# Gated expert rows added onto the residual in DRAM by an accumulating scatter, and a last stage that only normalises

## The reference

```
x = layernorm(x + rotor_attention(x))      # values, turned, running sum, turned back, projected
x = layernorm(x + decayed_attention(x, ctx, ctx))
x = layernorm(x + moe(x))

def moe(x):                                # 8 experts, 2 chosen per row
    probs = softmax(x @ router.T); scores, idx = top_k(probs, 2)
    scores = scores / sum(scores)          # the gates of a row, sum 1
    out = 0
    for each chosen expert e:
        h = x @ up[e]                      # 256 -> 512
        hidden = silu(h[:, :256]) * h[:, 256:]
        out += scores[e] * (hidden @ down[e])
    return out
```

## Time and profile before

| | |
|---|---|
| time, median of 3 runs | 296.65 us (294.85 to 298.92) |
| span of the profiled execution | 269.3 us; the page gives no other time for it |
| busy: TensorE matmul, weight load | 208.4 us (77%), 184.8 us (69%) |
| busy: VectorE, GpSimd, ScalarE | 169.8 us (63%), 153.1 us (57%), 116.8 us (43%) |
| mean granted TensorE clock | 0.915 |
| DMA | 35.75 MB, mean 133 GB/s; read from HBM 27.12 MB, written 9.31 MB |

### The profile page before, as it was taken

How to read it: one execution, slowest core, us unless ns; L and a number is a source line. 1 busy time by engine, 2 the same in 40 slices (tenths; PEclk the granted TensorE clock), 3 DMA queues, 4 the chain that set the end, 5 groups by cost and what they waited for, 6 DMA issues and landing times.

```text
span 269.3 us, 5242 instructions
## 1 busy us (share of the span) xinstructions
PE 208.4 (77%) x1393; PEld 184.8 (69%) x1394; DVE 169.8 (63%) x534; ACT 116.8 (43%) x286; POOL 153.1 (57%) x140
## 2 busy tenths in 40 slices
PE   8387698988989998857899999999999999400000
PEld 8387587977978888757688888888888888300000
DVE  5945988889889768595355455455554554207993
ACT  4352251433424420381345545454554554515665
POOL 1264857747756720085567777777777774515330
PEclk9889999999999999995999999999999999855555
DMA  7945456656543100550223223233332332079413
GB/s 222 392 163 179 136 194 223 168 176 198 205 164 119 39 22 21 189 166 2 88 79 104 86 94 99 86 97 100 97 96 87 97 95 78 12 213 318 171 78 156
DMA packets 20130, 35.75 MB, mean 133 GB/s; under 512 B 2861, under 2 KB 11312, under 8 KB 20112
## 3 DMA queue, kind: packets, MB, share of 16 engines
q1 hardware_dynamic: 16368, 26.21, 29.6%
q0 software_dynamic: 3744, 9.31, 11.3%
HBM read 27.12 MB, written 9.31 MB: 135 GB/s over the span
## 4 chain that ended last, share of the span: by engine, by line
PE 62%; DVE 17%; issue 9%; POOL 4%; DMA 4%; ACT 2%; DVEq 1%; SPq 0%; ACTq 0%; POOLq 0%
PE p_c L558 13%; PE p_v L558 7%; PE p_y L480 6%; PE p_y L584 4%; PE p_r L558 4%; PE p_a L558 4%; PE p_s L464 3%; PE p_s L558 3%; PE p_v L420 3%; PE p_t L597 3%; POOL space L1020 3%; DVE space L851 3%; PE p_r L508 2%; PE p_a L499 2%; PE p_t L446 2%
## 5 line engine op out<-in xcount | busy, mean ns | idle before, releaser
L558 PE MATMUL p_c<-w_hi,parts 128*128 x104 | 34.6, 414 | 0.0
L1044 POOL DMA_INDIRECT y_dram<-x1T,scatter_now x26 | 26.3, 1013 | 11.8 <-issue 5.3
L1024 POOL DMA_INDIRECT turns<-x_dram,gather_now x26 | 25.4, 979 | 12.6 <-issue 3.8
L823 DVE TENSOR_TENSOR parts<-p_y,parts 128x256 fp32r<-128x256 f32 x39 | 16.5, 424 | 17.6 <-ACT parts L934 17.6
L1011 POOL TENSOR_TENSOR w_lo<-keep,w_hi 128x1536 fp32r<-128x1536 f32 (+1 forms) x8 | 27.5, 3434 | 0.1
L833 DVE TENSOR_TENSOR cs<-p_c,cs 128x256 f32<-128x256 f32 x26 | 11.0, 425 | 22.6 <-ACT cs L941 22.6
L994 POOL TENSOR_TENSOR space<-back 128x512 f32<-128x512 f32 x8 | 10.2, 1271 | 18.9 <-DVE back L717 18.9
L941 ACT ACTIVATE cs<-p_c 128x256 f32<-128x256 f32 x26 | 10.1, 387 | 24.6 <-PE p_c L558 24.6
L437 PE MATMUL p_c<-const,space 128*128 128x128 f32 x128 | 17.3, 292 | 4.2 <-DVE space L671 4.2
L664 DVE TENSOR_SCALAR x<-r,mv,rs 128x256 f32<-128x256 f32 x32 | 20.2, 671 | 0.6
L1002 POOL TENSOR_TENSOR cs<-space,vinv 128x256 f32<-128x256 f32 x16 | 9.5, 612 | 18.5 <-DVE vinv L731 15.0
(11 more groups left out here) (161 smaller groups left out, 575.0 us busy)
## 6 DMA issues: line engine op xcount, KB each, us to landing
keep<-in_weights SPq DMA_DIRECT2D x8, 768.0 KB, 4.4
space<-y_dram SPq DMA_DIRECT2D x16, 256.0 KB, 4.2
space<-in_xT SPq DMA_DIRECT2D x8, 256.0 KB, 3.5
keep<-in_x SPq DMA_DIRECT2D x8, 256.0 KB, 3.5
space<-in_ctxT SPq DMA_DIRECT2D x8, 256.0 KB, 2.8
space<-in_ctxt SPq DMA_DIRECT2D x8, 256.0 KB, 3.1
x_dram<-x SPq DMA_DIRECT2D x8, 256.0 KB, 2.2
keep<-x_dram SPq DMA_DIRECT2D x1, 2048.0 KB, 8.4
```

The source lines that it names most:

```text
L558: last = nc.tensor.matmul(dst, lhs[:, k, :], w[:].rearrange("p e n -> p (e n)")[:, bass.ds(start + col + k * width, width)], start=(n == 0 ...
L823: nc.vector.tensor_tensor(xs_lo[s], p_xt, xs_hi[s].bitcast(F32), ALU.subtract).then_inc(xlo_ok, 1)
L1024: nc.gpsimd.indirect_dma_start(xs[s], None, x2_dram, bass.IndirectOffsetOnAxis(ap=gather_now[s][:], axis=0)).then_inc(xs_ok[s], 16)
L1044: nc.gpsimd.indirect_dma_start(y_dram, bass.IndirectOffsetOnAxis(ap=scatter_now[s][:], axis=0), ys[s], None, bounds_check=TOPK * N - 1, oo ...
```

## The change

Each row that an expert yields is scaled by its gate as ScalarE copies it out of PSUM, and the scatter adds it (`compute_op=ALU.add`) onto a row of `sum_dram`, into which SP has written x2 as well; padding goes to 128 spare rows. For this:

- A row of `x2_dram` has 258 floats: x2 and the two gates of the token. SP stores x2 twice, to `x2_dram` and to `sum_dram`, and waits for both. The gates are stored by one DMA (`gate_rows`) after VectorE has computed them, and VectorE computes them before its row masks. GpSimd's gathers wait for that store.
- Per tile VectorE picks the gate: `min(max(first_pick, gate 2), gate 1)` with `first_pick` 2 for a first choice and 0 for a second; gate 1 is never the smaller one.
- Two tiles may hold the two choices of one token, so GpSimd waits before a scatter until the scatter of the tile before has landed (`put_ok`).
- The load of all of x2 into `keep` goes. The last stage loads eight tiles of 256 KB from `sum_dram`, issued at once, takes the statistics, and normalises one half on ScalarE and the other on GpSimd. Its loops are written out.

```diff
--- before.py
+++ after.py
...
@@ -112,14 +115,13 @@
 
 
         keep = sb("keep", [P, PAIRS * 2 * D])
-        x2_keep = keep[:].rearrange("p (j n) -> p j n", n=2 * D)
+        sums = keep[:].rearrange("p (j q d) -> p j q d", q=2, d=D)
         w_in = [keep[:, s * W_END:(s + 1) * W_END] for s in range(2)]
         x_in = [keep[:, 2 * W_END + s * 2 * D:2 * W_END + (s + 1) * 2 * D].rearrange("p (q d) -> p q d", q=2)
                 for s in range(2)]
 
 
-        space = sb("space", [P, PAIRS * TOPK * 2 * D])
-        y_all = space[:].rearrange("p (j c n) -> p j c n", j=PAIRS, c=TOPK)
+        space = sb("space", [P, SPACE])
         taken = [8 * 2 * D]
 
         def part_of_space(words, dt=F32):
...
@@ -212,15 +217,16 @@
         expert_idx = sb("expert_idx", [P, TILES], I32)
 
 
-        xs = [turns[:, 0, :], turns[:, 1, :], rem[:, 0, :]]
+        xs = [sb(f"xs{s}", [P, ROW]) for s in range(RING)]
         xs_hi, xs_lo, hid_hi, hid_lo = ([parts[:, RING * n + s, :, :] for s in range(RING)] for n in range(4))
         silu, hid = cs[:, 0, :], cs[:, 1, :]
         ys = [x1T[:, 0, :, :].rearrange("p k t -> p (k t)"), x1T[:, 1, :, :].rearrange("p k t -> p (k t)"), x2T[:, 0, :, :].rearrange("p k t -> p (k t)")]
 
-        x2_dram = nc.dram_tensor("x2_dram", (N, D), F32, kind="Internal").ap()
-        y_dram = nc.dram_tensor("y_dram", (TOPK * N, D), F32, kind="Internal").ap()
-        x2_pairs = x2_dram.rearrange("(j q t) d -> j t q d", q=2, t=T)
-        y_pairs = y_dram.rearrange("(c j q t) d -> c j t q d", c=TOPK, q=2, t=T)
+        x2_dram = nc.dram_tensor("x2_dram", (N, ROW), F32, kind="Internal").ap()
+        sum_dram = nc.dram_tensor("sum_dram", (N + P, D), F32, kind="Internal").ap()
+        x2_pairs = x2_dram.rearrange("(j q t) d -> j t q d", q=2, t=T)[:, :, :, 0:D]
+        gate_rows = x2_dram.rearrange("(b t) d -> t b d", t=T)[:, :, D:D + TOPK]
+        sum_pairs = sum_dram[0:N, :].rearrange("(j q t) d -> j t q d", q=2, t=T)
 
         p_v = ps("p_v", [P, 2, D])
         p_c = ps("p_c", [P, 2, 2, D])
...
@@ -353,6 +354,8 @@
                     sp.wait_ge(x2_ok, i - 1)
                     sp.dma_start(x2_pairs[bass.ds(i - 2, 1), :, :, :].rearrange("a t q d -> t (a q) d"),
                                  x2[s][:]).then_inc(x2_out[s], 16)
+                    sp.dma_start(sum_pairs[bass.ds(i - 2, 1), :, :, :].rearrange("a t q d -> t (a q) d"),
+                                 x2[s][:]).then_inc(x2_out[s], 16)
                 if has(1):
                     if has(-1):
                         sp.wait_ge(sc_ok, i)
@@ -361,7 +364,7 @@
                         sp.wait_ge(cs_ok, i)
                     load(c_in, ctxt, c_ok, i + 1, 1 - s)
                 if has(-2):
-                    sp.wait_ge(x2_out[s], 8 * (i - s))
+                    sp.wait_ge(x2_out[s], 16 * (i - s))
                     sp.sem_inc(x2_free, 1)
 
             sp.sem_inc(x2_free, 2)
@@ -375,29 +378,17 @@
             sp.dma_start(half[:], halves).then_inc(half_in, 16)
             pipeline(sp, step, 0)
             sp.sem_inc(x2_saved, 1)
-
-            sp.dma_start(x2_keep.rearrange("p j n -> p (j n)").rearrange("p (j q d) -> p (j q) d", q=2, d=D),
-                         x2_dram.rearrange("(j t) d -> t j d", t=T)).then_inc(x2_back, 16)
-
+            sp.wait_ge(gate_ok, 1)
+            sp.dma_start(gate_rows, gate[:]).then_inc(gates_saved, 16)
 
             for s in range(RING):
                 sp.wait_ge(put_ok[s], 16 * (TILES // RING))
-
-            def load_rows(j):
-                for c in range(TOPK):
-                    sp.dma_start(y_all[:, j, c, :].rearrange("p (q d) -> p q d", q=2), y_pairs[c, j]).then_inc(
-                        y_back[j], 16)
-
-            for j in range(AHEAD):
-                load_rows(j)
             for j in range(PAIRS):
-                sp.wait_ge(y_back[j], 32)
-                sp.sem_inc(y_in_ok, 1)
-                if j + AHEAD < PAIRS:
-                    load_rows(j + AHEAD)
+                sp.dma_start(sums[:, j, :, :], sum_pairs[j]).then_inc(sum_back[j], 16)
             for j in range(PAIRS):
                 sp.wait_ge(res_ok, j + 1)
-                sp.dma_start(out[j], y_all[:, j, 1, :]).then_inc(out_ok, 16)
+                sp.wait_ge(res2_ok, j + 1)
+                sp.dma_start(out[j], sums[:, j, :, :].rearrange("p q d -> p (q d)")).then_inc(out_ok, 16)
             sp.wait_ge(out_ok, 16 * PAIRS)
 
         @block.tensor
@@ -788,6 +779,11 @@
                                          ALU.is_equal))
             codes = half[:, H_CODE:H_CODE + TOPK * B].unsqueeze(2).to_broadcast([P, TOPK * B, TILES])
             nc.vector.tensor_tensor(tile_hot, tile_is, codes, ALU.mult).then_inc(tile_hot_ok, 1)
+            dve.wait_ge(exp_ok, 1)
+            link(nc.vector.tensor_tensor(tsum[:], expd[:, 0, :], expd[:, 1, :], ALU.add))
+            link(nc.vector.reciprocal(tinv[:], tsum[:]))
+            nc.vector.tensor_tensor(gate[:], expd[:].rearrange("p c b -> p b c"),
+                                    tinv[:].unsqueeze(2).to_broadcast([P, B, TOPK]), ALU.mult).then_inc(gate_ok, 1)
             dve.wait_ge(row_no_ok, 1)
             for n in DVE_ROWS:
                 nc.vector.tensor_scalar(row_hot[:, n, :], half[:, H_ROW:H_ROW + P], row_no[:, n:n + 1], None,
@@ -804,16 +800,11 @@
                                          upto[3][:, E:].unsqueeze(1).to_broadcast([P, TILES, E]), ALU.is_ge))
             link(nc.vector.tensor_reduce(expert[:], past, AX_X, ALU.add))
             nc.vector.tensor_scalar(expert_idx[:], expert[:], float(E - 1), float(W_END), ALU.min, ALU.mult).then_inc(index_ok, 1)
-            nc.vector.tensor_scalar(token[:], coded[:], -1.0, 0.0, ALU.add, ALU.max).then_inc(index_ok, 1)
-            nc.vector.tensor_scalar(second[:], code[:], 0.0, float(N), ALU.is_lt, ALU.mult).then_inc(index_ok, 1)
-            nc.vector.tensor_scalar(padding[:], code[:], 0.0, float(SKIP), ALU.is_equal, ALU.mult).then_inc(index_ok, 1)
-            dve.wait_ge(index_ok, 4)
-            link(nc.vector.tensor_tensor(coded[:], token[:], second[:], ALU.add))
-            link(nc.vector.tensor_tensor(scatter_idx[:], coded[:], padding[:], ALU.add))
-            dve.wait_ge(exp_ok, 1)
-            link(nc.vector.tensor_tensor(tsum[:], expd[:, 0, :], expd[:, 1, :], ALU.add))
-            link(nc.vector.reciprocal(tinv[:], tsum[:]))
-            nc.vector.tensor_tensor(gate[:], expd[:], tinv[:].unsqueeze(1).to_broadcast([P, TOPK, B]), ALU.mult).then_inc(gate_ok, 1)
+            nc.vector.tensor_scalar(first_pick[:], code[:], 0.0, FIRST, ALU.is_ge, ALU.mult).then_inc(index_ok, 1)
+            nc.vector.tensor_scalar(padding[:], code[:], 0.0, const[:, C_SPARE:C_SPARE + 1], ALU.is_equal,
+                                    ALU.mult).then_inc(index_ok, 1)
+            dve.wait_ge(index_ok, 3)
+            link(nc.vector.scalar_tensor_tensor(scatter_idx[:], coded[:], -1.0, padding[:], ALU.add, ALU.add))
 
 
             def tile(k, at, has):
@@ -821,6 +812,8 @@
                     s, _ = at(1)
                     dve.wait_ge(xhi_ok, k + 2)
                     nc.vector.tensor_tensor(xs_lo[s], p_xt, xs_hi[s].bitcast(F32), ALU.subtract).then_inc(xlo_ok, 1)
+                    nc.vector.tensor_scalar(gate_at[:, bass.ds(k + 1, 1)], first_pick[:, bass.ds(k + 1, 1)],
+                                            xs[s][:, D + 1:D + 2], xs[s][:, D:D + 1], ALU.max, ALU.min).then_inc(gate_at_ok, 1)
                 if has(4):
                     s, _ = at(1)
                     nc.vector.tensor_copy(gather_now[s][:], gather_idx[:, bass.ds(k + 4, 1)]).then_inc(gather_now_ok, 1)
@@ -844,33 +837,22 @@
             tile_pipeline(dve, tile)
 
 
-            def finish(i, s, has):
-                if has(0):
-                    dve.wait_ge(sum0_ok, i + 1)
-                    for q in range(2):
-                        last = nc.vector.scalar_tensor_tensor(
-                            y_pair(i, 0)[:, q, :], y_pair(i, 1)[:, q, :], gate[:, 1, bass.ds(2 * i + q, 1)],
-                            y_pair(i, 0)[:, q, :], ALU.mult, ALU.add)
-                    last.then_inc(r3_ok, 1)
-                if has(-1):
-                    dve.wait_ge(sd3_ok, i)
-                    nc.vector.reciprocal(rs_pair[1 - s][:], sd_pair[1 - s][:]).then_inc(rs3_ok, 1)
-                if has(0):
-                    dve.wait_ge(r3_ok, i + 1)
-                    dve.sem_inc(carried, 1)
-                    for q in range(2):
-                        nc.vector.bn_stats(st_pair[s][:, q, :], y_pair(i, 0)[:, q, :]).then_inc(st3_ok, 1)
-                if has(-1):
-                    dve.wait_ge(rs3_ok, i)
-                    nc.vector.scalar_tensor_tensor(shift[1 - s][:], mv_pair[1 - s][:, :, 0], -1.0, rs_pair[1 - s][:],
+            for j in range(PAIRS + 1):
+                if j < PAIRS:
+                    dve.wait_ge(sum_back[j], 16)
+                    for q in range(2):
```

(76 more changed lines are left out.)

33 lines of the change are left out of this document (18 added, 15 removed).

## The result

The changed kernel takes 346.65 us (344.43 to 348.16, four runs) against 297.78 us (294.85 to 299.26) for the kernel before on the same chip, a ratio of 1.166 with an interval of 1.1575 to 1.1745. It is slower by 49 us. The forecast was 343 us. As the experiments show, the total is near partly by luck: its base and its main term were wrong by 26 and 27 us, with opposite signs. The times given are medians over all executions of a kernel, and the ratios are taken over its fast ones alone, those within 1.5% of its fastest.

The account below looks back on a forecast made before the run. The prediction took TensorE and GpSimd as both full in the tile stage. Its terms, 57.9 + 1.1 - 13.1 + 0.7 = +46.6 us on the median of 296.65, gave 343 us, range 310 to 385 us.

Parts of the forecast that it names:

- base: Starting point: profiled span of 269.3 us, median 296.65 us, the 27.35 us between carried over; tile interval 2.517 us.
- main term: Tile stage: scatters in a row, each waiting for the one before, period 4.04 against 2.517 us, +57.9 us.
- Term 1: Tile stage: waiting scatters lengthen the period to 4.04 us, +57.9 us; last landing +1.1 us later.
- first piece: Tile stage: start of an accumulating scatter to its landing, taken as 3.2 us, bounds 2.5 and 5.05.
- Second piece: Tile stage: from release of GpSimd to the start of the next scatter, taken as 0.84 us.
- Term 2: Last stage: loads, weighting and adding removed, VectorE setting the pace, 20.2 us against 33.30 us, -13.1 us.
- Term 3: Ahead of the gathers: computing and storing the gates first delays them 0 to +3 us, taken as +0.7 us.
- The edits at no cost: Second store of each pair, longer gathered rows, VectorE's gate selection, ScalarE's wait and scale, unskipped padding: no cost expected.
- (a): Tile stage: accumulation costs nothing over a plain write, period 3.34 us, +19 us, 316 us; chance 0.17.
- (b): Tile stage: TensorE's clock falls and matmuls lengthen, some 4.6 us a tile, +68 us, 364 us; chance 0.12.
- (c): Tile stage: accumulating scatter lands after 4.3 us and more, period 5.1 to 5.9, +100, 396 us; chance 0.12.
- (d): Ahead of the scatter: the wait does not bind, period about 2.6 us, -9 us, 287 us; chance 0.04.

Follow-up runs that it names:

- e2: Changed kernel with a plain indirect write in place of the accumulating scatter, wait kept; 294.03 us, ratio 0.9899 to the kernel before.
- e10: Changed kernel with the accumulating scatter of only 128 of each row's 256 columns; 326.12 us, ratio 1.0999 to the kernel before.
- e3: Changed kernel with three sums in DRAM, one per ring slot, and no wait for the neighbouring scatter; 281.36 us, ratio 0.9453 to the kernel before.
- e7: Changed kernel, everything computed, with two sums for even and odd tiles, scatters waiting two tiles back; 285.36 us, ratio 0.9642 to the kernel before.
- the second trace: Kernel before, unchanged, profiled again; the profiled execution took 299.01 us with a span of 297.2 us.
- e9: Kernel before with one unused GpSimd addition of 128x256 ahead of every scatter; 292.51 us, ratio 0.9866.
- e11: Changed kernel with GpSimd normalising its half for the first four pairs only, ScalarE doing the rest; 341.66 us, ratio 1.1431 to the kernel before.
- e8: Changed kernel with six more 128x1 copies per tile on VectorE, with semaphore increments; 349.23 us against 346.65.
- after: The changed kernel itself, against the kernel before; 346.65 us, ratio 1.166.
- e12: Kernel before with one unused GpSimd memset of 128x16 after ScalarE's last normalisation; 301.13 us, ratio 1.0107.

## Why the total was right and the steps were not

**The mechanism of the change was right.** The wait takes over the tile stage, the cycle is landing plus wake-up, TensorE falls to two thirds busy, and the last stage is shorter by a dozen microseconds.

**Term 1, first piece: mis-sized.** "I take 3.2 us" for the landing, near the lower end of 2.5 to 5.05; it is 3.8. The reason given, that the new thing is only the read of DRAM at no more than 0.85 us, failed: the packets doubled and the extra is 1.3 us (e2), of which at least 0.7 is not bytes (e10). The instruction's own growth to 1.59 us was not foreseen; it runs inside the landing here and cost nothing, but in e3 and e7 it is what sets the pace. **Second piece:** 0.84 was 0.93, since the waits for two semaphores follow the landing. The cycle was to be 4.04 and is 4.749: 38 x 0.71 = 27 us too little.

**The base: wrong.** "What lies between, 27.35 us, is start and end of a launch and is carried over unchanged." It is 1.8 us. The other 25.5 us are ScalarE's standstills (26.4 us by the intervals), which the second trace shows and the first one has not; that the other executions have them too follows from their spans alone. The changed kernel has none, as is to be expected of one whose wait slows the tiles beyond 3.2 us (e9). Against ordinary executions the interval term is (4.749 - 3.213) x 38 = +58.4 us, where the forecast had 57.9; against the execution profiled first it is (4.749 - 2.517) x 38 = +84.8. Too short a cycle and too quick a base, 27 and 26 us, cancelled. That was luck: with the ordinary interval of 3.213 us as its base the same cycle gives (4.04 - 3.213) x 38 = +31 us, and a forecast of some 317 us.

**Term 2: -13.1 forecast, -12.0 measured**, and again by errors that cancel. To the second pair's load 5.2 us where 3.4 were set; statistics and normalising, 0.93 + 8.49 us from 327.92 to 337.34, where 12.7 + 0.3 + 1.3 were set, as shifts cost 170 ns and not 380 and GpSimd and VectorE overlap; and 6.7 us after the last arithmetic, where 2.5 were. The prediction looked for GpSimd's price as an engine (0.9 to 1.8 us a pair; it is 1.23), not for what follows its last instruction: e11's span shows that giving it the last pairs cost about 4.5 us.

**Term 3: 0, not +0.7.** The store landed 0.9 us before it was needed. The edits at no cost were free within what the traces show: the first gather starts at 126.04 us, in the two traces of the kernel before at 126.03 and 127.36, and the added selection on VectorE disappears in slack that six more copies don't fill (e8).

**The rivals.** (a), accumulation for the price of a write, is what e2 shows: had it held, the time would have been 294 us, level with the kernel before, and not the 316 that the wrong base gave. (b): the clock did fall, to 0.82 over the stage, with TensorE busy for 67%, but TensorE is not in the cycle, so its matmuls' length didn't count. (c) was the right direction from 3.2, not the size. (d): the wait binds, by a wide margin. It is made not to bind by moving the neighbour two tiles away (e7), which no rival considered.

## What to carry to other kernels

Before a span is set against a median, profile the kernel twice, and compare the difference of span and time between kernels: a gap of 27 us is not a launch. A wait on a transfer in a loop costs landing plus wake-up against the interval, so look first how many intervals can lie between the two ends: a second destination turned 4.75 us a tile into 3.18 at an unchanged landing of 3.8. And the engine that closes a stage is chosen also by what comes after its last instruction; GpSimd was the wrong one here.

## What the runs showed that was not expected

- An accumulating indirect DMA of 128 rows of 1 KB: instruction 1.59 us and landing 3.8 us, plain 0.99 to 1.02 and 2.5; at 512 bytes a row 1.59 and 3.2 to 3.4.
- ScalarE stands still for 1.5 to 3.9 us, with its inputs ready where this was looked into, every two or three tiles, in a loop of 2.6 us a tile, and in none of the eight kernels at 3.18 us or more (after, e2, e3, e7, e8, e9, e10, e11). A kernel became 1.3% quicker by 0.75 us of useless work per tile. The cause is open.
- The program ends no sooner than 6.6 to 6.7 us after GpSimd's last arithmetic, in all eight traces in which that comes late enough to be seen (after, e2, e3, e7, e8, e10, e11, e12).
